# One-head attention and adapters in the last layer of a four-layer kernel: ScalarE copies query and key ahead of the exponentials, VectorE picks and adds ahead of the norm

## The reference

```python
def _L3_attn_ref(x, W, b):
    ...
    qkv = jnp.einsum('btc,cd->btd', x, W) + b
    q, k, v = jnp.split(qkv, 3, axis=-1)
    scale = 1.0 / math.sqrt(DK)
    weights = jnp.einsum('btc,bTc->btT', q, k) * scale
    ...
    logits = jnp.where(mask == 0, jnp.float32(-9000000000000000.0), weights)
    attention = jax.nn.softmax(logits, axis=-1)
    values = jnp.einsum('btT,bTc->btc', attention, v)
    return values

def _L3_ffn_ref(x, base_W, base_b, disc_mu, disc_sigma, down_W, down_b, up_W, up_b, conv_W, conv_b):
    ...
    base = jnp.einsum('btd,od->bto', x, base_W) + base_b
    m1 = x.mean(axis=1)
    m2 = (x * x).mean(axis=1)
    inv_var = 1.0 / (disc_sigma * disc_sigma)
    losses = (jnp.einsum('bd,ed->eb', m2, inv_var) - 2.0 * jnp.einsum('bd,ed->eb', m1, disc_mu * inv_var) + jnp.sum(disc_mu * disc_mu * inv_var, axis=1)[:, None]) / D
    idx = jnp.argmin(losses, axis=0)
    Wd, bd = (down_W[idx], down_b[idx])
    ...
    h = jax.nn.relu(jnp.einsum('btd,bdr->btr', x, Wd) + bd[:, None, :])
    a = jnp.einsum('btr,brd->btd', h, Wu) + bu[:, None, :]
    y = jnp.einsum('btd,bod->bto', a, Wc) + bc[:, None, :]
    return base + y
    ...
    x = x + _L3_attn_ref(_layernorm(x, axis=-1), L3_attn_W, L3_attn_b)
    x = x + _L3_ffn_ref(_layernorm(x, axis=-1), L3_ffn_base_W, L3_ffn_base_b, L3_ffn_disc_mu, L3_ffn_disc_sigma, L3_ffn_down_W, L3_ffn_down_b, L3_ffn_up_W, L3_ffn_up_b, L3_ffn_conv_W, L3_ffn_conv_b)
```

## Time and profile before

| | |
|---|---|
| median of 3 runs | 6013.17 us (6010.93 to 6014.99) |
| profiled execution, its own time | 6008.89 us |
| its span | 6007.2 us, mean granted TensorE clock 0.966 |
| PE busy | 5516.8 us (92%) |
| DVE busy | 4177.6 us (70%) |
| ACT busy | 2809.3 us (47%) |
| POOL busy | 2256.1 us (38%) |

### The profile page before, as it was taken

One profiled execution on the slowest core, in us unless ns is written; L12 is line 12 of the kernel. 1 busy time (PEld: TensorE's weight loads), 2 busy tenths in 40 slices (PEclk: granted clock), 3 DMA queues, 4 the chain that ended last, 5 costly groups with the idle time before them and its releaser, 6 DMA issues. The chain is left out here.

```text
span 6007.2 us, 119421 instructions
## 1 busy us (share of the span) xinstructions
PE 5516.8 (92%) x37438; PEld 3426.2 (57%) x37453; DVE 4177.6 (70%) x9588; ACT 2809.3 (47%) x4608; POOL 2256.1 (38%) x3170
## 2 busy tenths in 40 slices
PE   7997999999999899999999999999997879886687
PEld 5664444444444477657775677567754456644564
DVE  6785666666666688658874788478846866578764
ACT  4554222222222355545555555555555655534354
POOL 6662000000001466436653666356623532153212
PEclk9998999999999899999999999999998999898899
DMA  4333333333333555325542555055510000000002
GB/s 134 107 105 103 97 96 95 98 97 96 97 97 100 142 159 156 87 79 158 156 127 59 141 159 158 27 150 157 157 33 5 0 7 0 1 4 0 2 0 64
DMA packets 526333, 527.07 MB, mean 88 GB/s; under 512 B 55698, under 2 KB 436705, under 8 KB 503780
## 3 DMA queue, kind: packets, MB, share of 16 engines
q1 hardware_dynamic: 517684, 517.90, 31.5%
q10 hardware_dynamic: 8320, 5.25, 0.4%
HBM read 337.88 MB, written 185.07 MB: 87 GB/s over the span
## 5 line engine op out<-in xcount | busy, mean ns | idle before, releaser
L1121 DVE TENSOR_REDUCE a_mx<-a_unit 128x2 f32<-128x512 f32 (+1 forms) x1536 | 1033.9, 688 | 309.1 <-PE a_unit L1412 303.6
L1261 ACT ACTIVATE a_prob<-a_slot 128x1536 f32<-128x1536 f32 x512 | 742.9, 1451 | 550.1 <-PE a_slot L1435 464.8
L2098 ACT ACTIVATE f_silu<-f_pG 128x512 f32<-128x512 f32 x528 | 314.7, 597 | 935.1 <-PE f_pG L2182 921.1
L1410 PE MATMUL a_unit<-a_sk,a_sq 96*128 96x128 bf16 (+1 forms) x4096 | 597.5, 249 | 42.4 <-DMA a_sk<-a_kscratch 26.7
L2033 DVE TENSOR_TENSOR f_gated<-f_spread,f_silu 128x512 f32<-128x512 f32 x512 | 362.9, 709 | 341.2 <-ACT f_silu L2098 296.6
L2150 PE MATMUL f_pO<-f_hidden,f_wd 128*128 128x512 f32 x1056 | 546.3, 599 | 14.1 <-DVE f_hidden L2035 13.5
L60 POOL TENSOR_SCALAR f_veps<-f_moments 128x4 f32<-128x4 f32 (+1 forms) x112 | 25.3, 226 | 1420.1 <-DVE f_moments L1909 1020.4
L2182 PE MATMUL f_pG<-f_xnT,f_wg 128*128 128x512 f32 x1056 | 541.6, 594 | 0.0
L2186 PE MATMUL f_pU<-f_xnT,f_wu 128*128 128x512 f32 x1056 | 540.7, 594 | 0.0
L1412 PE MATMUL a_unit<-a_maskq,identb 128*128 128x256 bf16 (+1 forms) x1536 | 481.7, 314 | 2.1 <-issue 2.1
L1063 POOL TENSOR_SCALAR_AFFINE_SELECT a_prob<-a_prob 128x512 f32<-128x512 f32 x384 | 244.5, 637 | 519.4 <-ACT a_prob L1261 506.1
(11 more groups left out here) (473 smaller groups left out, 12165.1 us busy)
## 6 DMA issues: line engine op xcount, KB each, us to landing
f_spread<-f_scratch SPq DMA_DIRECT2D x1024, 128.0 KB, 2.9
a_sq<-a_qscratch SPq DMA_DIRECT2D x128, 768.0 KB, 5.6
a_sk<-a_kscratch SPq DMA_DIRECT2D x160, 384.0 KB, 6.6
a_qscratch<-a_parts SPq DMA_DIRECT2D x288, 192.0 KB, 2.2
a_qscratch<-a_parts SPq DMA_DIRECT2D x288, 128.0 KB, 2.2
a_kscratch<-a_parts SPq DMA_DIRECT2D x160, 192.0 KB, 2.2
a_kscratch<-a_parts SPq DMA_DIRECT2D x160, 128.0 KB, 2.2
a_qscratch<-a_parts SPq DMA_DIRECT2D x288, 64.0 KB, 1.8
```

The costliest lines, as they stand in the source:

```text
L1121: v.tensor_reduce(dst, src, op=ALU.max, axis=AX.X, negate=True).then_inc(red_done, 1)
L1261: act.activation(prob[gr % 2][:, :], slot[:, :], ACT.Exp, scale=SCALE).then_inc(exp_done, 1)
L1410: pe.matmul(bank[:, at * wide:(at + 1) * wide], q, sk[b][0:KM, gr * GH + h, 0:wide], start=(at == 0), stop=False)
L2098: act.activation(silu[c % 2][:, :], pG[c % 2][:, :], ACT.Silu).then_inc(silu_done, 1)
```

## The change

On ScalarE the two copies of query and key of sequence n+2 stand ahead of the exponentials of n+1 instead of behind them. They wait for a semaphore of their own, `qk_pe`, which TensorE raises behind the query and key projections; the value's users wait for `v_pe`, raised behind the value projections. In the adapters VectorE's `ln_apply` of n+4 stands behind the pick of n+3 and the add of n-1 instead of ahead of them. Nothing is computed otherwise.

```diff
@@ -3072,9 +3072,9 @@
         prob = [k.sb(f"prob{b}", [P, 3 * P]) for b in range(2)]; probT = k.sb("probT", [P, 3 * P])
         pT = k.ps("pT", [P, BLK]); pQK = k.ps("pQK", [P, BLK]); pV = k.ps("pV", [P, BLK])
         pS = [k.ps(f"pS{b}", [P, BLK]) for b in range(2)]; pP = k.ps("pP", [P, BLK]); pO = k.ps("pO", [P, BLK])
-        (w_in, apart, stats_done, rstd_done, xn_done, t_pe, xnT_done, qkv_pe, qk_done, val_done, s_pe, max_done,
+        (w_in, apart, stats_done, rstd_done, xn_done, t_pe, xnT_done, qk_pe, v_pe, qk_done, val_done, s_pe, max_done,
          exp_done, pt_pe, probT_done, o_pe, x_done) = k.sem(
-            "w_in apart stats_done rstd_done xn_done t_pe xnT_done qkv_pe qk_done val_done s_pe max_done "
+            "w_in apart stats_done rstd_done xn_done t_pe xnT_done qk_pe v_pe qk_done val_done s_pe max_done "
             "exp_done pt_pe probT_done o_pe x_done")
         COLS = [(0, 0, P), (1, P, 3 * P)]
@@ -3132,7 +3132,7 @@
                                                          op0=ALU.mult, op1=ALU.add)
                         ins.then_inc(x_done, 1)
                     if is_seq(n + 2):
-                        v.wait_ge(qkv_pe, n + 3)
+                        v.wait_ge(v_pe, n + 3)
                         v.tensor_tensor(val[b][:, :, :], pV[:, 0:SEQ].rearrange("p (t d) -> p t d", d=D),
                                         bv[:, :].unsqueeze(1).broadcast_to((P, QT, D)), op=ALU.add).then_inc(val_done, 1)
                     v.drain()
@@ -3149,13 +3149,19 @@
                     if is_seq(n + 2):
                         act.wait_ge(t_pe, n + 3)
                         if is_seq(n + 1):
-                            act.wait_ge(qkv_pe, n + 2)
+                            act.wait_ge(v_pe, n + 2)
                         act.activation(xnT[:, :], pT[:, 0:SEQ], ACT.Copy).then_inc(xnT_done, 1)
                     if is_seq(n):
                         act.wait_ge(pt_pe, n + 1)
                         if is_seq(n - 1):
                             act.wait_ge(o_pe, n)
                         act.activation(probT[:, :], pP[:, 0:3 * P], ACT.Copy).then_inc(probT_done, 1)
+                    if is_seq(n + 2):
+                        act.wait_ge(qk_pe, n + 3)
+                        if is_seq(n + 1):
+                            act.wait_ge(s_pe, n + 2)
+                        act.activation(q[:, :], pQK[:, 0:SEQ], ACT.Identity, bias=bqk[:, 0:1])
+                        act.activation(key[:, :], pQK[:, SEQ:2 * SEQ], ACT.Identity, bias=bqk[:, 1:2]).then_inc(qk_done, 1)
                     if is_seq(n + 1):
                         act.wait_ge(max_done, n + 2)
                         if is_seq(n - 1):
@@ -3165,12 +3171,6 @@
                             ins = act.activation(prob[nb][:, lo:hi], pS[nb][:, lo:hi], ACT.Exp, bias=negm[:, t:t + 1],
                                                  scale=SCALE, accum_out=ssum[nb][:, t:t + 1])
                         ins.then_inc(exp_done, 1)
-                    if is_seq(n + 2):
-                        act.wait_ge(qkv_pe, n + 3)
-                        if is_seq(n + 1):
-                            act.wait_ge(s_pe, n + 2)
-                        act.activation(q[:, :], pQK[:, 0:SEQ], ACT.Identity, bias=bqk[:, 0:1])
-                        act.activation(key[:, :], pQK[:, SEQ:2 * SEQ], ACT.Identity, bias=bqk[:, 1:2]).then_inc(qk_done, 1)
                 order(act, step)
             @block.tensor
@@ -3210,12 +3210,13 @@
                             pe.wait_ge(qk_done, n + 2)
                             pe.wait_ge(val_done, n + 2)
                         for c in range(2):
-                            pe.matmul(pQK[:, c * SEQ:(c + 1) * SEQ], wqkv[:, c * D:(c + 1) * D], xnT[:, :],
-                                      start=True, stop=True)
+                            ins = pe.matmul(pQK[:, c * SEQ:(c + 1) * SEQ], wqkv[:, c * D:(c + 1) * D], xnT[:, :],
+                                            start=True, stop=True)
+                        ins.then_inc(qk_pe, 1)
                         for t in range(QT):
                             out = pV[:, t * D:(t + 1) * D]
                             ins = pe.matmul(out, xnT[:, t * P:(t + 1) * P], wqkv[:, 2 * D:3 * D], start=True, stop=True)
-                        ins.then_inc(qkv_pe, 1)
+                        ins.then_inc(v_pe, 1)
                     if is_seq(n):
                         pe.wait_ge(probT_done, n + 1)
                         pe.wait_ge(val_done, n + 1)
@@ -3325,11 +3326,6 @@
                         link(v.tensor_tensor(muiv[:, :], mu[:, :], iv[:, :], op=ALU.mult))
                         v.tensor_scalar(cross[:, :], muiv[:, :], -2.0, None, ALU.mult)
                         v.tensor_tensor(square[:, :], muiv[:, :], mu[:, :], op=ALU.mult).then_inc(disc_done, 1)
-                    if is_seq(n + 4):
-                        v.wait_ge(rstd_done, n + 5)
-                        if is_seq(n + 3):
-                            v.wait_ge(t_pe, n + 4)
-                        ln_apply(v, rows(core["x"], (n + 4) * QT, QT), moments, rstd, xn).then_inc(xn_done, 1)
                     if is_seq(n + 3):
                         v.wait_ge(l_pe, n + 4)
                         link(v.tensor_scalar(gain[:, :], pL[0:1, 0:E], -1.0 / (D * SEQ), None, ALU.mult))
@@ -3340,6 +3336,11 @@
                         v.wait_ge(r_pe, n)
                         v.tensor_tensor(dst, pR[:, 0:SEQ].rearrange("p (t d) -> p t d", d=D), dst, op=ALU.add
                                         ).then_inc(x_done, 1)
+                    if is_seq(n + 4):
+                        v.wait_ge(rstd_done, n + 5)
+                        if is_seq(n + 3):
+                            v.wait_ge(t_pe, n + 4)
+                        ln_apply(v, rows(core["x"], (n + 4) * QT, QT), moments, rstd, xn).then_inc(xn_done, 1)
                     v.drain()
                     if is_seq(n + 5):
                         ln_stats(v, chain, rows(core["x"], (n + 5) * QT, QT), stats, moments, stats_done)
```

## The result

The changed kernel took 5992.51 us (median of 8 runs, 5980.23 to 5998.84), the kernel before 6013.4 beside it (8 runs, 6004.0 to 6016.56). The ratio is 0.996, with a 95% interval of 0.9951 to 0.997, so 18 to 29 us less, with 24 at its middle; the medians differ by 20.9. The forecast was 5996.1 in a range of 5986 to 6009.

A forecast was written before the change was run, and what follows sets the result against it. Taken as bounds: ScalarE's copy order in attention, VectorE's ring with GpSimd in the adapters. Attention -10.0 and adapters -7.1 make -17.1, from the profiled 6008.89 to 5991.8, or 5996.1 from the median 6013.17; range 5986 to 6009.

The forecast's parts named there:

- rival "more": Both loops gain more: VectorE needs 8.15 a pair in attention, adapters 3.45 a step; -24.5, 5989 us; chance .12.
- The 8.5: Attention's loop: forecast us per pair of steps after the change, down from 9.21; 13 pairs make -9.2.
- VectorE's 8.10: Attention's loop: VectorE's us per pair once its 14.4 us of waits for P·V are taken out.
- TensorE's own 8.01: Attention's loop: us per pair TensorE alone needs once its 15.6 us of waits for the key are taken out.
- Exponentials behind the key copy: Attention's loop: exponentials end at about 5779.3, transposes of probabilities come at 5779.7; .4 to spare, so no cost.
- -.3 and -.3: Attention ahead of its loop: -.3 for the one step there, -.3 for the first exponential's table load against earlier scores.
- The adapters' ring: Adapters' loop: distances, gain, add, normalize, transposes, next distances sum to 3.60 a step; 20 steps make -8.0.
- I charged 1.1: Adapters: +1.1 us, counted at half, in the sum of -7.1; part of its derivation is cut from the text.
- Attention only (6003): Adapters gain nothing: pick, distances and squares chain up to about 4.0 a step; 6003 us; chance .12.
- adapters only (6006): Attention gains nothing: VectorE or the late exponentials hold its pair near 9.2; 6006 us; chance .10.
- The delayed pick: Adapters' loop: VectorE's pick must stand aside until GpSimd's root ends, .34 more a step, 6.8 in all; 6003; chance .11.
- The low clock: Adapters: TensorE pauses every step and its clock stays at the lower level, 4.58 a step; slower, 6023 us; chance .05.

The follow-up runs named there:

- attention only: The kernel before with only attention's three edits, its adapters left as they were; 6004.61 us, ratio 0.998 to the kernel before.
- the two runs apart: Kernel before with only attention's edits, 6004.61 us (0.998), and kernel before with only the moved `ln_apply`, 6004.11 us (0.9976).

## Why the prediction held

**The total.** The ratio puts the gain at 18 to 29 us, the forecast was 17.1. By the medians it is 20.9, between the forecast and the 24.5 of the rival "more"; the ratio's middle, 24, is all but that rival's number. The range held it, but the forecast itself was too small: 17.1 lies below the interval. By stage, where the clock's rise is alike, attention gained 11.8 (1.9, 9.6 and .3) for a forecast of 10.0, the adapters 12.4 to 13.2 (.2, 11.4 and .8 to 1.6) for 7.1. So the mechanism of both parts came true, and most of the shortfall is in the adapters. (The bounds of the two loops, 14.4 and 14, add up to 28, not to the 25 that I gave for the range.)

**What bounds attention: right.** The wait for the key and the wait for P·V went, the query copy starts where it was placed, VectorE is the next limit. The loop gained 9.6 for a forecast of 9.2. The 8.5 had been put together from VectorE's 8.10 and .17 of dispatch kept twice, 8.44; it shows in the rows as `<-issue`, .21 and .19, and moving its values away brought the loop to 102.4. TensorE's own 8.01 was too high as a limit: the loop went down to 7.81 a pair without the value bias. So subtracting a wait doesn't give a floor to the tenth; why TensorE needs less than 8.01 no run shows.

**Exponentials behind the key copy, costed at nothing: right.** Transposes of the probabilities don't appear among the waits of the loop.

**The first steps of attention: missed in size.** The forecast gave them -.3 and -.3. Their two parts: from the first load to the first scores .86 less in the changed kernel (11.45 against 12.31), because the key copy no longer waits for the value projections while TensorE's clock is at .50; and from there to sequence 3 another 1.0 less with the clock's rise at 18 in both, 2.6 less with the rise at 12. I had costed these steps by the loop's gain, at a granted clock of 1.00. At .50 the value projections that the copies no longer wait for last 1.06 instead of .61. The table load is on the path now, as forecast; the exponential follows it at .02, as closely as in the earlier trace rows.

**The adapters' ring: right in its links, 5% too long.** 3.60 was forecast, 3.43 measured. Add to normalize is .34, not .44 (the value that the trace hadn't shown, below its lower bound of .35), transposes to distances 1.36 to 1.45, not 1.47. That is 3.4 us over 20 steps, the largest error of a term but for the clock's: the loop gained 11.4, not 8.0. The number is that of the rival "more", 3.45 a step; attention's loop stayed where the forecast had it, at 8.47 and not at that rival's 8.15.

**The clock in the adapters: wrong place.** I charged 1.1 to loop steps at a granted clock of .50, as in the earlier trace rows. No run shows that term: with the new order the adapters' loop ran at 1.00 in every trace, at 3.43 a step in both of the changed kernel. What the clock did cost lay ahead of the loop: it rose at 32 instead of 21 us, and the first steps took 3.5 longer in the old order and 4.5 in the new (40.87 against 37.36, 41.61 against 37.12). The dip that I charged isn't a mark of the old order either: in "attention only", whose adapters are the old ones, the loop ran at 1.00 too:

```profile
5895.40:5975.47 80.07, 67.55 (x364) 35.62 (x364) 44.11 (x221) 43.36 (x141) 21.76 (x60) 1.00 0.27 75
```

With the rise at 21 in both, the first steps are .24 shorter than before (37.12 against 37.36), where I had added .4. The steps behind the loop gained 1.6, not .6, but .75 of that came in "attention only" as well (24.23 against 24.98), so the order's share is .8 to 1.6.

**Rivals.** Attention only (6003) and adapters only (6006) fell with the two runs apart. The delayed pick fell: maximum and index kept their times (.16, then .08 and .15, the maximum lying inside the root in the changed kernel). The low clock fell: 1.00 in the loop. That TensorE's higher share, 97%, kept it up isn't shown, for the old order had 1.00 with 84%.

**Open.** What makes the granted clock rise at 12 or 18 us in attention and at 26 or 32 in the adapters, with the same program; and where the 12 us of spread ahead of attention arise. Neither was tried.

## What to carry to other kernels

When a step's period is a ring across engines, list its links with their times and take the next ring from the same list: here the period after the change came out 5% below that sum. The longest wait in a list need not be the cause; move it, and see whether the period follows. When work is moved to an idle engine, look at what it will lie beside: the same add cost .3 a step beside one instruction and next to nothing beside the other (7.88 a pair with it, 7.81 without). And compare loops, not spans, when the part that you changed is a twentieth of the kernel.

## What the hardware showed that I had not expected

GpSimd's 128x256 add lengthened VectorE's normalize (128x128, SBUF to SBUF, two in a row) from .60 to .80 and 1.00, but not the multiply-add of the same size that reads PSUM, .61 with it and without. The clock's rise moved by 6 us between two runs of the same program, worth 2.4 us in the adapters (41.61 against 39.25) and 1.6 in attention (24.07 against 25.65).
